# One gate product, norms inside the projections and averages inside the levels of a delta stage, and a layer norm in two parts

## The reference

```python
# cross attention and the norm behind it
x = _layernorm(x + ca, g2, be2)
# delta part; 4 heads of 128, short_conv has 4 taps
q = silu(silu(short_conv(h @ Wq, conv_q)));  k = silu(silu(short_conv(h @ Wk, conv_k)))
v = silu(short_conv(h @ Wv, conv_v))
beta = sigmoid(h @ Wb);  gamma = sigmoid(h @ Wdec)
mix = sigmoid(silu(short_conv(h @ Wmix, conv_mix)) + mix_bias)
q = l2norm(q);  k = l2norm(k);  v_b = v * beta;  k_b = k * beta
attn = inverse of (I + strict_lower(k_b @ k.T))     # per chunk, by rows
u = attn @ v_b;  w = attn @ k_b
# over chunks:  u_adj = u - w @ S;  o = q @ S + lower(q @ k.T) @ u_adj;  S = S + k.T @ u_adj
# running average over time:  s = gamma * s + (1 - gamma) * v
o = (1 - mix) * o + mix * s;  out = rms_norm(o, rms_w) @ Wo
```

## Time and profile before

| what | value |
|---|---|
| median of 3 runs | 1717.47 us (1717.05 to 1717.78) |
| the profiled execution | 1723.14 us |
| its span | 1721.9 us |
| mean granted TensorE clock | 0.949 |
| TensorE, VectorE, ACT, GpSimd busy | 92%, 56%, 44%, 21% |
| cross attention, about | 190 to 1064 us |
| feed-forward, about | 1064 to 1184 us |
| delta stage, about | 1184 to 1384 us |
| experts, about | 1384 to 1722 us |

### The profile page before, as it was taken

One profiled execution on the slowest core, in us unless ns is written; L12 is line 12 of the kernel. 1 busy time (PEld: TensorE's weight loads), 2 busy tenths in 40 slices (PEclk: granted clock), 3 DMA queues, 4 the chain that ended last, 5 costly groups with the idle time before them and its releaser, 6 DMA issues.

```text
span 1721.9 us, 31727 instructions
## 1 busy us (share of the span) xinstructions
PE 1585.8 (92%) x12972; PEld 1307.9 (76%) x12972; DVE 962.0 (56%) x1363; ACT 762.9 (44%) x1186; POOL 360.1 (21%) x257
## 2 busy tenths in 40 slices
PE   7858999999999999999999996995889679999998
PEld 3645999999998999989999985882379466666665
DVE  4482444444444444444454465436955668888885
ACT  1113445445454454454544543440412036666664
POOL 1012323223232232232322330402124100000000
PEclk9878999999999999999999998997969879999999
DMA  6001222121221212211221207106000008999992
GB/s 219 1 0 37 77 65 66 54 66 50 66 66 54 63 53 66 66 52 54 65 65 54 87 29 279 48 0 220 0 1 5 21 10 299 349 332 344 346 347 99
DMA packets 114264, 179.74 MB, mean 104 GB/s; under 512 B 5440, under 2 KB 54592, under 8 KB 113600
## 3 DMA queue, kind: packets, MB, share of 16 engines
q1 hardware_dynamic: 114112, 177.60, 30.9%
HBM read 176.53 MB, written 1.05 MB: 103 GB/s over the span
## 4 chain that ended last, share of the span: by engine, by line
PE 85%; DVE 10%; issue 2%; POOL 1%; ACT 1%; DMA 0%; DVEq 0%; ACTq 0%; POOLq 0%
PE ring L609 17%; PE ring L600 17%; PE ring L1811 8%; PE sc L626 6%; PE turnbank L639 5%; PE pv L1835 4%; PE pv L655 4%; PE sc L1109 3%; PE pv L1811 3%; PE sc L1508 2%; PE pv L1843 2%; PE ring L1118 1%; PE sc L372 1%; DVE stat L163 1%; PE ring L1508 1%
## 5 line engine op out<-in xcount | busy, mean ns | idle before, releaser
L538 POOL TENSOR_TENSOR x_l<-raw,x_h 128x1024 fp32r<-128x1024 f32 x96 | 239.9, 2499 | 606.2 <-ACT x_h L532 606.1
L848 DVE TENSOR_TENSOR kT<-ring,kT 64x512 fp32r<-64x512 f32 (+1 forms) x224 | 141.6, 632 | 266.2 <-ACT kT L736 264.6
L609 PE MATMUL ring<-wv_h,x_h 128*128 128x256 f32 (+1 forms) x832 | 243.6, 293 | 0.2 <-DVE kT L848 0.2
L600 PE MATMUL ring<-x_h,wk_h 128*128 128x256 f32 (+1 forms) x768 | 230.3, 300 | 8.3 <-POOL x_l L538 7.8
L609 PE MATMUL ring<-wv_l,x_h 128*128 128x256 f32 (+1 forms) x832 | 234.3, 282 | 0.0
L609 PE MATMUL ring<-wv_h,x_l 128*128 128x256 f32 (+1 forms) x832 | 233.9, 281 | 0.0
L600 PE MATMUL ring<-x_h,wk_l 128*128 128x256 f32 (+1 forms) x768 | 220.8, 287 | 0.0
L600 PE MATMUL ring<-x_l,wk_h 128*128 128x256 f32 (+1 forms) x768 | 220.6, 287 | 0.0
L1660 DVE TENSOR_TENSOR w_lo<-w_raw,w_hi 128x2048 fp32r<-128x2048 f32 x88 | 200.4, 2284 | 25.0 <-ACT w_hi L1901 25.0
L736 ACT CAST kT<-ring 64x512 fp32r<-64x512 f32 (+1 forms) x224 | 120.1, 536 | 202.0 <-PE ring L600 200.5
L532 ACT CAST x_h<-raw 128x1024 fp32r<-128x1024 f32 x96 | 103.9, 1084 | 170.5 <-PE ring L609 170.3
(11 more groups left out here) (431 smaller groups left out, 2901.1 us busy)
## 6 DMA issues: line engine op xcount, KB each, us to landing
w_raw<-in_ew SPq DMA_DIRECT2D x96, 1024.0 KB, 5.8
raw<-in_ctxT SPq DMA_DIRECT2D x80, 512.0 KB, 3.7
raw<-in_ctxT SPq DMA_DIRECT2D x16, 642.0 KB, 4.0
wf<-in_wf SPq DMA_DIRECT2D x2, 4096.0 KB, 14.6
xin<-in_x SPq DMA_DIRECT2D x1, 1024.0 KB, 5.6
w_in<-in_wq SPq DMA_DIRECT2D x1, 1024.0 KB, 8.0
w_in<-in_wk SPq DMA_DIRECT2D x1, 1024.0 KB, 10.2
w_in<-in_wv SPq DMA_DIRECT2D x1, 1024.0 KB, 12.3
```

Of the source, the lines that this page charges most:

```text
L538: pool.tensor_tensor(x_l[:, k, :, 0:w], raw[:, k, :, 0:w], x_h[:, k, :, 0:w].bitcast(F32), ALU.subtract)\
L600: m = pe.matmul(ring[k % 2][:, j * w:j * w + w], wt[:, c, e:e + P], xt[:, s, c, 0:w], start=c == 0 and n == 0, stop=c == NC - 1 and n == 2)
L609: m = pe.matmul(ring[k % 2][0:r, j * G:(j + 1) * G], xt[:, s, c, t0:t0 + r], wt[:, c, h * G:(h + 1) * G], start=c == 0 and n == 0, stop=c ...
L848: ins = dve.tensor_tensor(lo, src, hi.bitcast(F32), ALU.subtract)
```

## The change

- Gates: one product with a weight block of 68 columns, the three gates at columns 0, 32 and 64, into bank 4, in place of three products into three banks. The weight array is padded with zeros on the host and has a new place in SBUF.
- Behind projection 8 TensorE spreads gamma for heads 0 and 1 and turns the gates; behind projection 10 it spreads gamma for heads 2 and 3 and sums the squares of k. ACT copies the spread gammas in its iterations 9 and 11.
- The running averages move on VectorE to the ends of levels 1 to 4. They read ACT's copy of gamma and use a buffer of their own (`egv`).
- Gram blocks go ahead of the turned values, in other banks. ACT and no longer VectorE scales the turned values, in four pieces per tile.
- xm and xmT are made by tile. GpSimd's first level mask and the y products wait by tile; the qk masks come after all of them, and the third and fourth y and the first two w wait for qk masks.
- Last cross sequence: `dve_x_b` (bias, statistics, center) moves ahead of the third turned copy of a round, and `dve_x_b_end` (shift) ends the round.

The core of the diff (removed bodies that stand in the listing above are cut):

```diff
+            if link is not None:
+                dve_x_b(dve, link, p)
             dve_turned(dve, b, p, 2)
             if before is not None:
                 dve_cross_add(dve, b - 1, before[0], before[1])
...
             if jobs is not None:
                 dve_job(dve, nb, nh, jobs + 2)
             if link is not None:
-                dve_x_b(dve, link, p)
+                dve_x_b_end(dve, p)
...
         norm_stats(dve, link, xa, t)
-        norm_affine(dve, link, 2, xa, xa, t, rows4[:, 0, :], rows4[:, 1, :]).then_inc(sem("normed"), 1)
+        dve.wait_ge(sem("variance_ready"), norm_count(2, t))
+        link(norm_center(dve, xa, t, rows4[:, 0, :]))
+    def dve_x_b_end(dve, t):
+        norm_shift(dve, 2, xa, xa, t, rows4[:, 1, :]).then_inc(sem("normed"), 1)
...
-    wgates = at("wgates", S0 + 192, [P, NC, 12])
+    wgates = at("wgates", R + 210752, [P, NC, 64 + GH])
+    egv = at("egv", R + 212800, [P, TOK])
...
+    gram_bank = (4, 5, 0, 1)
+    turn_bank = (2, 3, 6, 7)
...
-            if l == 1:
-                pool.wait_ge(sem("nT_ready"), NT)
-                pool.wait_ge(sem("transposed_n"), NT)
-                pool.wait_ge(sem("xm_started"), 1)
-            else:
+            if l > 1:
                 pool.wait_ge(sem("y_done"), NT * (l - 1))
             for t in range(NT):
+                if l == 1:
+                    pool.wait_ge(sem("nT_ready"), t + 1)
+                    pool.wait_ge(sem("xm_started"), 2 * t + 1)
...
-        dve.wait_ge(sem("gates_done"), 3)
+        dve.wait_ge(sem("gates_done"), 1)
...
         for n in range(NPROJ + 2):
+            if n == 10:
+                dve.wait_ge(sem("gates_turned"), 1)
+                dve.tensor_copy(gtok[:, :, :, :].rearrange("p a t h -> p (a t h)"), bank[7][:, 0:2 * NM])\
+                   .then_inc(sem("gtok_ready"), 1)
+            if n == NPROJ:
+                norms_out(0)
...
-        norms_out(0)
...
         for t in range(NT):
-            dve.wait_ge(sem("v_turned"), t + 1)
-            dve.tensor_tensor(four3(vtok, t), bank3(4 + t), factor(1, t), ALU.mult).then_inc(sem("vtok_ready"), 1)
-        for t in range(NT):
             dve.wait_ge(sem("gram_done"), t + 1)
-            dve.tensor_tensor(four3(nT_s, t), bank3(t), factor(0, t), ALU.mult).then_inc(sem("n_ready"), 1)
-        dve.wait_ge(sem("n_ready"), NT)
+            dve.tensor_tensor(four3(nT_s, t), bank3(gram_bank[t]), factor(0, t), ALU.mult).then_inc(sem("n_ready"), 1)
         dve.wait_ge(sem("masks_ready"), 1)
-        link(dve.tensor_tensor(tbuf[:, :, :], nT_s[:, :, :], over_tiles(mask1[:, :], NM), ALU.mult))
-        link(dve.tensor_tensor(xm[:, :, :], over_tiles(ident[:, :], NM), tbuf[:, :, :], ALU.subtract))
-        dve.wait_ge(sem("nT_ready"), NT)
-        link(dve.tensor_tensor(tbuf[:, :, :], nT_all[:, :, :], over_tiles(masks[:, 0, :], NM), ALU.mult))
-        dve.tensor_tensor(xmT[:, :, :], over_tiles(ident[:, :], NM), tbuf[:, :, :], ALU.subtract).then_inc(sem("xm_started"), 1)
+        for t in range(NT):
+            dve.wait_ge(sem("n_ready"), t + 1)
+            link(dve.tensor_tensor(four3(xm, t), four3(nT_s, t), over_tiles(mask1[:, :], 4), ALU.mult))
+            dve.tensor_tensor(four3(xm, t), over_tiles(ident[:, :], 4), four3(xm, t), ALU.subtract).then_inc(sem("xm_started"), 1)
+            dve.wait_ge(sem("nT_ready"), t + 1)
+            link(dve.tensor_tensor(four3(xmT, t), four3(nT_all, t), over_tiles(masks[:, 0, :], 4), ALU.mult))
+            dve.tensor_tensor(four3(xmT, t), over_tiles(ident[:, :], 4), four3(xmT, t), ALU.subtract).then_inc(sem("xm_started"), 1)
         for t in range(NT):
             dve.wait_ge(sem("qk_done"), t + 1)
-            dve.tensor_tensor(four3(qk, t), bank3(t), over_tiles(incl[:, :], 4), ALU.mult).then_inc(sem("qk_ready"), 1)
+            dve.tensor_tensor(four3(qk, t), bank3(turn_bank[t]), over_tiles(incl[:, :], 4), ALU.mult).then_inc(sem("qk_ready"), 1)
         norms_out(1)
-        dve.wait_ge(sem("xm_started"), 1)
...
+        def running_average(h):
+            dve.wait_ge(sem("gamma_used_a"), h + 1)
+            dve.wait_ge(sem("ema_ready") if h else sem("values_ready"), h or NC)
+            link(dve.scalar_tensor_tensor(egv[:, :], four(tbuf, h), 1.0, vf[:, h, :], ALU.subtract, ALU.mult))
+            link(dve.memset(tbuf[:, 4 * h:4 * h + 4, :].rearrange("p m w -> p (m w)")[:, 0:TOK:S], 0.0))
+            dve.tensor_tensor_scan(ema[:, h, :], four(tbuf, h), egv[:, :], 0.0, ALU.mult, ALU.subtract)\
+               .then_inc(sem("ema_ready"), 1)
...
+            running_average(l - 1)
...
-            act.wait_ge(sem("gates_done"), i + 1)
-            act.activation(g[:, :], bank[4 + i][0:GH, :], ACT.Tanh, scale=0.5).then_inc(sem("gate_tanh"), 1)
+            act.wait_ge(sem("gates_done"), 1)
+            act.activation(g[:, :], bank[4][32 * (i + 1):32 * (i + 1) + GH, :], ACT.Tanh, scale=0.5).then_inc(sem("gate_tanh"), 1)
...
-        for h in range(GH):
-            act.wait_ge(sem("gamma_spread"), h + 1)
-            act.wait_ge(sem("gamma_used_v"), h + 1)
-            act.copy(four(tbuf, h), bank[h]).then_inc(sem("gamma_used_a"), 1)
+            if n in (9, 11):
+                for h in ((0, 1) if n == 9 else (2, 3)):
+                    act.wait_ge(sem("gamma_spread"), h + 1)
+                    act.copy(four(tbuf, h), bank[4 + h % 2]).then_inc(sem("gamma_used_a"), 1)
         for t in range(NT):
             act.wait_ge(sem("transposed_n"), t + 1)
-            act.copy(four(nT_all, t), bank[4 + t]).then_inc(sem("nT_ready"), 1)
+            act.copy(four(nT_all, t), bank[gram_bank[t]]).then_inc(sem("nT_ready"), 1)
+            act.wait_ge(sem("v_turned"), t + 1)
+            act.wait_ge(sem("factors_ready"), 2)
+            for m in range(4 * t, 4 * t + 4):
+                ins = act.activation(vtok[:, m, :], bank[turn_bank[t]][:, level_matrix(m)], ACT.Copy, scale=scal[:, 1, m:m + 1])
+            ins.then_inc(sem("vtok_ready"), 1)
...
-        for i in range(3):
-            for c in range(NC):
-                k = pe.matmul(bank[4 + i][0:GH, :], wgates[:, c, GH * i:GH * (i + 1)], xT[:, c, :], start=c == 0, stop=c == NC - 1)
-            k.then_inc(sem("gates_done"), 1)
+        for c in range(NC):
+            k = pe.matmul(bank[4][0:64 + GH, :], wgates[:, c, :], xT[:, c, :], start=c == 0, stop=c == NC - 1)
+        k.then_inc(sem("gates_done"), 1)
+        def sum_squares(i):
+            pe.wait_ge(sem("squares_ready"), i + 1)
+            for m in range(NM):
+                k = pe.matmul(bank[6 - 2 * i][:, m:m + 1],
+                              squares[i][:, m % GH, (m // GH) * P:(m // GH + 1) * P], ones[:, 0:1], start=True, stop=True)
+            k.then_inc(sem("norms_done"), 1)
+        def spread_gamma(h):
+            if h >= 2:
+                pe.wait_ge(sem("gamma_used_a"), h - 1)
+            pe.matmul(bank[4 + h % 2], sel[:, h, :], gamma[:, :], start=True, stop=True).then_inc(sem("gamma_spread"), 1)
...
+            if n == 8:
+                pe.wait_ge(sem("gates_ready"), 3)
+                pe.wait_ge(sem("masks_ready"), 1)
+                spread_gamma(0)
+                spread_gamma(1)
+                for i, g in enumerate((beta, mixr)):
+                    for t in range(NT):
+                        k = pe.transpose(bank[7][:, (i * NT + t) * GH:(i * NT + t + 1) * GH], g[:, t * P:(t + 1) * P],
+                                         ident[0:GH, 0:GH])
+                k.then_inc(sem("gates_turned"), 1)
+            if n == 10:
+                spread_gamma(2)
+                spread_gamma(3)
+                sum_squares(0)
...
+        pe.wait_ge(sem("feature_ready"), NC)
+        for t in range(NT):
+            if t < 2:
+                pe.wait_ge(sem("gamma_used_a"), 3 + t)
+            else:
+                pe.wait_ge(sem("conv_done"), 7 + t)
+            each(gram_bank[t], t, lambda m: tile(kf, m), lambda m: tile(kf, m), "gram_done")
+        pe.wait_ge(sem("values_ready"), NC)
+        pe.wait_ge(sem("conv_done"), NPROJ)
+        for t in range(NT):
+            if t == 2:
+                pe.wait_ge(sem("norms_summed"), 1)
+            elif t == 3:
+                pe.wait_ge(sem("gtok_ready"), 1)
+            turn(turn_bank[t], t, lambda m: tile(vf, m), "v_turned")
+        for t in range(NT):
+            pe.wait_ge(sem("n_ready"), t + 1)
+            turn(gram_bank[t], t, lambda m: nT_s[:, m, :], "transposed_n")
         pe.wait_ge(sem("feature_ready"), 2 * NC)
...
         for t in range(NT):
             pe.wait_ge(sem("vtok_ready"), t + 1)
-            pe.wait_ge(sem("n_ready"), t + 1)
-            turn(4 + t, t, lambda m: nT_s[:, m, :], "transposed_n")
-        for t in range(NT):
-            each(t, t, lambda m: tile(kf, m), lambda m: tile(qf, m), "qk_done")
-        for t in range(NT):
-            pe.wait_ge(sem("nT_ready"), t + 1)
+            each(turn_bank[t], t, lambda m: tile(kf, m), lambda m: tile(qf, m), "qk_done")
```

(8 more changed lines are left out.)

56 lines of the change are left out of this document (11 added, 45 removed).

## The result

Before: 1717.52 us, median of 4 runs (1717.05 to 1717.78). After: 1700.97 us, median of 4 (1697.72 to 1702.50). Ratio 0.9899, 95% interval 0.9881 to 0.9916: 16.6 us faster by the medians (17.3 by the ratio, 14.4 to 20.4), inside the range, 5 us above the forecast of 1696.0.

A forecast was written before the change was run, and what follows sets the result against it. TensorE, busy 92% of the span, was taken as bound, with time won only where it waits or runs throttled. Terms -21.5 (first w) + 1.0 + 0.8 - 1.8 = -21.5 from 1717.5 gave 1696.0 us; range 1689.5 to 1702.5.

The forecast's parts named there:

- the projections: Delta stage behind the gates: 41.2 us of projections plus 7.9 of spreads, turns and sums; the last ends at 1240.9.
- Gate product: Start of the delta stage: one product of 8 matmuls takes 5.1 us, so the projections start 6.6 us earlier.
- rival 2: Clock falls in more places, at spreads and sums or at the w products: 4 us more, 1700; chance 0.18.
- To the factors: From norm sums (1245.3) over GpSimd and factors: VectorE starts scaling Gram blocks at 1249.3, against 1271.8 before.
- Masks per tile: VectorE's 16 instructions for xm and xmT take 11.3 us, plus 5.0 colliding with GpSimd's masks: done at 1268.2.
- rival 1: GpSimd's masks don't collide with VectorE's xmT instructions: 5.0 us more gain, 1691; chance 0.12.
- First w: Milestone, start of the first level's w products: 1270.9 against 1292.48, 21.5 us earlier.
- Clock gap, 1.0: TensorE's gap of some 4 us before the third y product lowers the clock: 1.0 us lost (0 to 3.5).
- Fourth average, 0.8: The fourth running average stands ahead of the r1 copies: TensorE waits 0.8 us (0 to 1.5).
- Cross unit, 1.8: Last cross unit, layer norm in two parts around the turned copy: 1.8 us gained (0.8 to 2.8).
- Frame: Trace differences are subtracted from the median, 1717.47; against the profiled execution's 1723.14 the forecast is 5.67 us higher.
- Range: Whole kernel: 1689.5 (no mask collision, full cross gain) to 1702.5 (falling clock and unhidden averages, outer ends of 1.0 and 0.8).

The follow-up runs named there:

- the second profile: The changed kernel, unchanged, run and profiled once more beside the kernel before: 1700.71 us, ratio 0.9896.
- the last kernel above, with everything: After plus 128-column sums, sums of k behind the last projection, PSUM reads beside GpSimd's masks, first average in the factors' wait, others in levels 1 to 3: 1693.73 us.
- the two edits of the sums: Two separate kernels against after: sums of squares of k moved behind the last projection, 1696.89 us; sums as products of 128 columns, 1699.14 us.
- 128 columns alone: After with each 128x1 product of the sums of squares made 128x128, same order and place: 1699.14 us, ratio 0.9882.
- both edits of the sums: After with sums of squares as products of 128 columns and the sums of k behind the last projection, together: 1698.52 us, ratio 0.9888.

## Why the prediction was right, and where it was off

Direction and range held, and most mechanisms that it named; the 5 us between forecast and result are almost all one term, the projections. By its own steps, counted from the start of the gates:

- **Gate product**: 5.1 us forecast, 6.2 measured. The start moved forward, the clock did not: it was 0.50 up to about 1189, so 5 us of the product ran at half clock and not 3.4. Where the gates started at 1186.7 they took 5.02 us, as forecast (the last kernel above). VectorE's first convolution came at 1197.48, 13.7 us behind the gates, where 12.6 had been forecast. That TensorE is the bound here and each matmul counts is shown (three products: 7.0 us).
- **The projections** are the step that failed. 49.1 us forecast from the end of the gates to that of the last projection, 54.6 measured. "Sums of squares 3.63 us at full clock" was too low for the sums (4.33, and 6.22 in the second profile) and wrong for what stands behind them: the last projection took 6.4 us instead of 3.5. Projections 9 and 10 took 8.77 instead of 7.1, since the clock was at 0.50 from 1223 to 1226.5, right behind the first spreads and small turns; this is so in four of the eleven profiles with this order of the projections (8.7 to 8.8 us), in the others the clock held there and they took 7.1, and nothing here tells why. The forecast reckoned only with idle gaps as a cause of a low clock. The earlier trace rows could not have told it: there the clock fell 1.7 us behind the sums of q, in the wait of 2.83 us. This is rival 2 (0.18), near its size of 4 us and at its 1700, and its place was half right: the sums ran partly at half clock, the spreads (1.98 us for 4) did not, only what stood behind them. Shown for the last projection by the two edits of the sums: 3.7 and 3.6 us.
- **To the factors**: 3.4 us forecast from VectorE's last product to the scaling, 3.8 measured. Three averages lie free in the levels, and putting all four back costs 7.1 us.
- **Masks per tile**: 4.07 us a tile forecast, 3.60 measured. The collision is there, so rival 1 is out, but it costs 0.95 us a tile and not 1.25, since GpSimd starts its mask late itself (1.58 for 1.27) and VectorE waits only for the rest. That gave back 1.9 us.
- **First w**: 84.2 us forecast, 88.9 and 88.5 measured, 4.7 late: 0.9 from the gates, 5.5 from the projections, 0.4 from the factors, less 2.1 from there to the first w, mostly the masks.
- **Clock gap, 1.0**: absent in after (0.50 us of waiting, first w 1.09), because TensorE was too slow to have a gap. With the sums repaired it is there in some profiles: 1.2 us with 128 columns alone, 1.6 with everything, none with both edits of the sums.
- **Fourth average, 0.8**: 0.4.
- **Cross unit, 1.8**: right in kind, 1.2 us by the same two instructions in fourteen profiles, inside its 0.8 to 2.8. The ratio of the medians says 4.1 (1.4 to 6.7), the start of the gates 3.8 in the mean of twelve profiles, with a spread as wide as the effect. In the trace of after VectorE's centering is held by GpSimd's split twice (1.88 and 2.56 us for 0.75) and the shift once (2.78), and TensorE's busy time rises by 1.0.
- **Frame**: differences of the trace taken from the median. It held: 16.5 us in the delta stage and 1.2 in the cross unit are 17.7, and the medians say 16.6, the ratio 17.3. The profiles' 21.3 have 3.6 us more, ahead of the last cross unit, between it and the gates and behind the output projection, and in these places the second profile of after differs from the first by as much and more. What in them makes the 5.6 us by which before's profiled execution lay above its median, no run showed.
- **Range**: its ends don't follow quite from what they name. Rival 1 with a cross gain of 2.8 gives 1690.0 and not 1689.5, and 1702.5 holds rival 2 with the outer ends, not rivals 2 and 3 together. The result of 1701 needed neither.

## What to carry to other kernels

Look at what a matmul does to the ones behind it: a cheap-looking block of one-column products can leave the clock low for the dense work that follows, so place it where the next work does not matter, or give it columns. Where two engines exclude each other over SBUF, order the instructions so that the one with an operand in PSUM runs beside the other, and first see that the engine so relieved is the bound. And before a gain seen between two profiles is set against medians, cut the profile at fixed instructions and see how much the rest varies by itself.

## What the runs showed of the hardware

- The granted clock fell from 1.00 to 0.50 while TensorE was shown busy without a gap: in 32 matmuls of 128x1 (1236 to 1238 and 1264 us in after, and in its second profile, where the sums took 6.22 us and the last projection 6.17), in all eight profiles of the new order with one column; and in four of eleven behind four matmuls over 4 partitions and eight of 4x4 (1223 us in after). With 128x128 in place of 128x1 it stayed at 1.00 through the sums in all three profiles, and they took 3.7 to 3.8 us. It fell behind waits too: 1.86 us in after, 2.06 and 3.41 with 128 columns alone.
- In the earlier trace rows and here 32 matmuls of 128x1 and of 128x128 take the same time at full clock, 3.63 and 3.73 us.
- Executions differ by up to 7 us in places that the change does not touch: the gates start at 1179.4 to 1186.7 us with the same instructions ahead, and the rest of the span is 1537.8 to 1544.9 us over the fourteen profiles. Behind the output projection it is 356.1 to 356.3 us in three of them and 358.0 to 359.3 in eleven; one kernel, after, has both (356.1 and 359.1).
